# Cross-attention kernel, layer 0: rankings one head pair later, token blocks split straight from PSUM, the output product ahead of the values

## What is computed

```python
score = jnp.einsum('bqhd,bkhd->bhqk', h_q, h_k)
score = score + position_bias[None]
score = jnp.where(m, score, -jnp.inf)
score = jax.nn.softmax(score, axis=-1)
score = jnp.where(m, score, 0.0)
attn = jnp.einsum('bhqk,bkhd->bqhd', score, h_v).reshape(b, lq, H * DH)
out = attn @ w_out.T
return hidden_states + out
```

## Time and profile before

| what | value |
|---|---|
| median of 3 runs | 1880.85 us (1878.38 to 1881.03) |
| profiled execution, own time | 1878.18 us |
| its span in the profile | 1876.3 us |
| mean granted PE clock | 0.985 |
| busy PE / DVE / ACT / POOL | 1791.9 / 1415.9 / 653.5 / 690.5 us |

### The profile page before, as it was taken

One profiled execution on the slowest core, in us unless ns is written; L12 is line 12 of the kernel. 1 busy time (PEld: TensorE's weight loads), 2 busy tenths in 40 slices (PEclk: granted clock), 3 DMA queues, 4 the chain that ended last, 5 costly groups with the idle time before them and its releaser, 6 DMA issues. The chain is left out here.

```text
span 1876.3 us, 29528 instructions
## 1 busy us (share of the span) xinstructions
PE 1791.9 (95%) x10312; PEld 1510.3 (80%) x10312; DVE 1415.9 (75%) x2838; ACT 653.5 (35%) x1785; POOL 690.5 (37%) x457
## 2 busy tenths in 40 slices
PE   7789999999999999997999998879999999999998
PEld 5679889888888988896776664666888888888886
DVE  6777777777777777776536876779778888888886
ACT  5222223333223212332114766531343343343333
POOL 6633344443334343432223002426433333334331
PEclk9989999999999999999999998989999999999999
DMA  3121011111110111120010001110101010100111
GB/s 143 42 72 48 31 50 50 50 50 50 50 50 23 49 40 40 50 77 1 23 45 20 1 26 56 35 42 21 46 25 44 34 34 34 34 34 34 34 35 46
DMA packets 32026, 78.27 MB, mean 42 GB/s; under 512 B 4096, under 2 KB 10944, under 8 KB 31584
## 3 DMA queue, kind: packets, MB, share of 16 engines
q1 hardware_dynamic: 31968, 77.50, 12.6%
HBM read 75.39 MB, written 2.10 MB: 41 GB/s over the span
## 5 line engine op out<-in xcount | busy, mean ns | idle before, releaser
L649 POOL TENSOR_TENSOR l0x_comb<-l0x_neg,l0x_bias 128x1024 f32<-128x1024 bf16 x32 | 70.2, 2194 | 375.4 <-DVE l0x_probs L1048 362.5
L945 ACT ACTIVATE l0x_probs_t<-bank 128x512 f32<-128x512 f32 x32 | 19.1, 597 | 527.5 <-PE bank L789 527.5
L2852 POOL TENSOR_TENSOR l3x_q<-l3x_q,l3x_cross 128x512 f32<-128x512 f32 x64 | 89.7, 1407 | 188.3 <-DVE l3x_q L1823 188.3
L37 PE MATMUL bank<-l0x_w_v_hi,ctx_hi 128*128 128x256 f32 x512 | 145.0, 283 | 0.0
L39 PE MATMUL bank<-l0x_w_v_hi,ctx_lo 128*128 128x256 f32 x512 | 145.0, 283 | 0.0
L38 PE MATMUL bank<-l0x_w_v_lo,ctx_hi 128*128 128x256 f32 x512 | 144.9, 283 | 0.0
L929 ACT ACTIVATE l0x_probs<-l0x_probs,l0x_top 128x129 f32<-128x129 f32 x256 | 99.4, 390 | 65.7 <-DVE l0x_top L1052 65.7
L37 PE MATMUL bank<-ctx_hi,l0x_w_k_hi 128*128 128x512 f32 x256 | 104.7, 409 | 8.3 <-DVE ctx_lo L1130 8.3
L3039 ACT ACTIVATE l3x_probs<-l3x_probs,l3x_top 128x128 f32<-128x128 f32 x256 | 99.1, 389 | 38.1 <-DVE l3x_top L3120 38.0
L1092 DVE TENSOR_TENSOR x<-x,bank 128x512 f32<-128x512 f32 x120 | 82.1, 684 | 37.5 <-PE bank L39 37.5
L37 PE MATMUL bank<-l3x_qin_hi,l3x_w_q_hi 128*128 128x512 f32 x256 | 105.7, 413 | 2.2 <-ACT l3x_v L3073 1.9
(11 more groups left out here) (486 smaller groups left out, 5358.4 us busy)
## 6 DMA issues: line engine op xcount, KB each, us to landing
l0x_raw_k<-L_k_dram SPq DMA_DIRECT2D x32, 256.0 KB, 3.3
l0x_raw_v<-L_v_dram SPq DMA_DIRECT2D x16, 512.0 KB, 3.3
l0x_raw_q<-L_q_dram SPq DMA_DIRECT2D x16, 512.0 KB, 4.2
l0x_raw_o<-L_o_dram SPq DMA_DIRECT2D x16, 512.0 KB, 3.4
l3x_raw<-L_q_dram SPq DMA_DIRECT2D x16, 512.0 KB, 3.2
l3x_raw<-L_o_dram SPq DMA_DIRECT2D x16, 512.0 KB, 3.3
kv_raw<-L_kv_dram SPq DMA_DIRECT2D x8, 512.0 KB, 3.4
l0x_ctx_raw<-ctx_t_dram SPq DMA_DIRECT2D x4, 512.0 KB, 6.0
```

What stands on the lines that cost most here:

```text
L37: pe.matmul(out, lhs[0], rhs[0], start=start, stop=False)
L649: pool.tensor_tensor(comb[:, :, :], neg[:, :, :], bias[:, j:j + 1, :].to_broadcast([P, B, P]), ALU.add).then_inc(comb_ready, 1)
L945: act.activation(probs_t[:, 0:BH, :], bank[6][:, :].rearrange("p (b n) -> p b n", b=BH), ACT.Copy).then_inc(t_act, 1)
L2852: pool.tensor_tensor(dst[:, part], dst[:, part], cross[n][:, :], ALU.add).then_inc(rotated, 1)
```

## The change

- **Rankings.** Pair 0 ranks no more. In pair p the ranking p-1 runs, and the last (15) goes into DVE's part of the feed-forward layer, a step behind each of the eight output tiles (`between(b)`).
- **Even step.** `project_out` stands ahead of the four `value_bank` on PE, and DVE's additions ahead of its value drains; the ranking's first round stands behind the second addition.
- **Blocks.** ACT rounds the transposed x from PSUM right into `xs[0]` (`high_x`), DVE copies the same bank to `xt` and subtracts the low part from PSUM (`copy_x`). The sums are made in another order, two (`T1`, `T2`) before pair 0, two within it; PE waits for two, then for four. Pair 0's queries have a buffer of their own (`raw_q0`), so that pair 1's are loaded at the start and split before pair 0. The mask is turned into `neg` by ACT.
- **Queues.** SP: the mask ahead of x; `load_work(p)` at the end of pair p, where `load_work(p + 1)` stood, and thus one in the last pair, too. ACT: in the last pair `w_o` is split ahead of `copy_probs(h)`.

The diff, cut:

```diff
@@ L0Ffn.vector
-    def vector(self, dve):
+    def vector(self, dve, between):
...
             core.statistics(dve, b)
+            between(b)
@@ l0_layer
-        ITEM = {"k_odd": 0, "v": 2, "out": 6, "p1": 14, ...
+        ITEM = {"k_odd": 0, "out": 2, "v": 10, "p1": 14, ...
-        SUMS = {3: 3, 4: 0, 5: 1, 6: 2}
+        T1, T2, T3, T4 = 4, 5, 3, 6
+        SUMS = {T1: 3, T2: 0, T3: 1, T4: 2}
@@ sync, period
                     if not last:
-                        if first:
-                            sp.wait_ge(ring_full, 10)
-                        else:
-                            sp.wait_ge(q_ready, p)
-                        load_q(p + 1)
+                        if not first:
+                            load_q(p + 1)
                         load_v(p + 1)
                         load_k(p + 1, 1)
                     if first:
-                        sp.wait_ge(xs_ready, L0_BLOCKS)
+                        sp.wait_ge(xs_ready, 4)
                     load_o(p)
                     if not last:
                         load_bias(p + 1, 0)
-                        load_work(p + 1)
+                    if not first:
+                        load_work(p)
@@ gpsimd
-                pool.tensor_scalar(neg[:, :, :], mask_u8[:, :, :], 1.0, -MASKED, ALU.subtract, ALU.mult
-                                   ).then_inc(neg_ready, 1)
                 pool.wait_ge(neg_ready, 1)
                 combine(0, 0)
-                for n in range(3):
-                    pool.wait_ge(xs_hi, n + 1)
-                    pool.tensor_tensor(xs[1][:, n, :, :], x_block(n), as_f32(xs[0][:, n, :, :]), ALU.subtract
-                                       ).then_inc(xs_ready, 1)
+                sum_queries(1)
+                low_queries(1)
@@ tensor, period
                     if not first:
+                        project_out(p - 1, at(p, "out"))
                         pe.wait_ge(v_ready, p + 1)
                         for m in range(4):
                             value_bank(at(p, "v") + m, 4, OUT_BANKS[m], m)
-                        project_out(p - 1, at(p, "out"))
...
-                    if first:
-                        pe.wait_ge(xs_ready, L0_BLOCKS)
                     pe.wait_ge(q_ready, p + 1)
                     block_product(at(p, "p1"), 3, 0, 0, 0)
-                    block_product(at(p, "p6"), 3, 3, 5, 5)
+                    if first:
+                        pe.wait_ge(xs_ready, 2)
+                    block_product(at(p, "p6"), 3, 3, 5, T2)
@@ scalar, period
                         for n in range(3):
                             ffn.high(act, n)
+                        split_high(p, raw_o, w_o, o_loaded, o_hi, at(p, "out") + B)
...
                     copy_probs(h)
@@ vector, before the pairs
+                def copy_x(b):
+                    dve.wait_ge(xt_hi, b + 1)
+                    dve.tensor_copy(xt[:, :, b * P:(b + 1) * P], bank[4 + b % BH][:, :].rearrange("p (c t) -> p c t", c=DC)
+                                    ).then_inc(xt_done, 1)
+                    tokens = slice(b % BH * P, (b % BH + 1) * P)
+                    if b < BH:
+                        dve.tensor_tensor(xs[1][:, 0:2, :, tokens], bank[4 + b][:, :].rearrange("p (k e t) -> p k e t", k=2, e=2),
+                                          as_f32(xs[0][:, 0:2, :, tokens]), ALU.subtract).then_inc(core.xt_copied, 1)
...
@@ vector, period
-                        rank_start(p)
+                        rank_start(p - 1)
+                        for m in range(4):
+                            add_out(at(p, "out"), 2 * m, OUT_BANKS[2 * m % 4])
+                            add_out(at(p, "out"), 2 * m + 1, OUT_BANKS[(2 * m + 1) % 4])
+                            rank_round(p - 1, m)
                         for m in range(4):
                             drain(at(p, "v") + m, OUT_BANKS[m], v[:, 2 * m:2 * m + 2, :])
                             if m < 3:
-                                rank_round(p, m)
-                        for m in range(4):
-                            add_out(at(p, "out"), 2 * m, OUT_BANKS[2 * m % 4])
-                            add_out(at(p, "out"), 2 * m + 1, OUT_BANKS[(2 * m + 1) % 4])
-                            rank_round(p, 3 + m)
-                        rank_end(p)
+                                rank_round(p - 1, 4 + m)
+                        rank_end(p - 1)
...
-                    step_odd(p)
+                    step_odd(p, first)
                     if first:
-                        rank_start(p)
-                        for r in range(ROUNDS + 1):
-                            rank_round(p, r)
-                        rank_end(p)
                         dve.wait_ge(h_added, B)
```

More of the change, by code:

```diff
@@ L509, in l0_layer @@
         heads = pair("heads", [P, 2, T])
-        probs = [sb("probs0", [P, B, P + 1]), sb("probs1", [P, B, P + 1])]
+        probs = [sb("probs0", [P, B, P + 1])]
+        with ExitStack() as early:
+            raw_q0 = core.sb(early, "l0x_raw_q0", [P, 2, DC, P])
+        probs.append(sb("probs1", [P, B, P + 1]))
         idle = sb("idle", [P, 1])
@@ L544, in at @@
             return PER * p - 2 + ITEM[what]
-        OUT_LAST = at(N - 1, "out") + B
+        OUT_LAST = at(N - 1, "v") + 4
         ADDED = OUT_LAST + 1
@@ L570, in load_q @@
                 def load_q(i):
+                    wait(sp, q_ready, i - 1)
                     sp.dma_start(raw_q[:, :, :, :], dram["L0_q"][i, :, :, :, :]).then_inc(q_loaded, 16)
@@ L703, in period @@
                     combine(p, 1)
-                    if not last:
-                        sum_queries(p + 1)
-                        split_low(p + 1, raw_k[0], w_k[0], k_hi[0], k_ready[0])
-                        low_queries(p + 1)
                     if first:
@@ L711, in period @@
                                            ).then_inc(core.rstd_done, 1)
-                        pool.wait_ge(lift_done, 2)
+                    if not last and not first:
+                        sum_queries(p + 1)
+                    if not last:
+                        split_low(p + 1, raw_k[0], w_k[0], k_hi[0], k_ready[0])
+                    if not last and not first:
+                        low_queries(p + 1)
                     if last:
@@ L754, in plain_query @@
                     for c in range(DC):
-                        mm = product(pe, bank[bk][:, :], [raw_q[:, j, c, :]], [xt[:, c, n * HALF:(n + 1) * HALF]],
+                        mm = product(pe, bank[bk][:, :], [raw_q0[:, j, c, :]], [xt[:, c, n * HALF:(n + 1) * HALF]],
                                      c == 0, c == DC - 1)
@@ L979, in _ @@
                     scale_x(b)
-                act.wait_ge(ctx_lo, DC)
+                act.wait_ge(mask_loaded, 16)
+                act.activation(neg[:, :, :], mask_u8[:, :, :], ACT.Copy, bias=MASKED, scale=-MASKED).then_inc(neg_ready, 1)
                 act.wait_ge(shift_done, 2)
@@ L983, in _ @@
                     scale_x(BH + b)
-                    copy_x(b)
+                    high_x(b)
                 split_high(0, raw_k[1], w_k[1], k_loaded[1], k_hi[1], 0)
-                high_x(0)
-                high_x(1)
                 for b in range(BH, B):
-                    copy_x(b)
-                for n in range(2, L0_BLOCKS):
-                    high_x(n)
+                    high_x(b)
+                high_queries(1, 0)
+                high_sum(T1, 1)
+                high_sum(T2, 2)
                 def period(p, first, last):
@@ L997, in period @@
                     exps(h, 0)
-                    if not first:
+                    if first:
+                        high_sum(T3, 3)
+                        high_sum(T4, 4)
+                    else:
                         heads_high(h - 1, 1)
@@ L1014, in period @@
                         split_high(p + 1, raw_v, w_v, v_loaded, v_hi, 6 if first else at(p, "v") + 4)
-                    split_high(p, raw_o, w_o, o_loaded, o_hi, 0 if first else at(p, "out") + B)
+                        split_high(p, raw_o, w_o, o_loaded, o_hi, 0 if first else at(p, "out") + B)
                 pairs(period, act)
@@ L1151, in _ @@
+                for b in range(BH):
+                    copy_x(b)
                 drain(5, 1, v[:, 6:8, :])
+                copy_x(4)
+                copy_x(5)
                 drain(6, 2, q00)
+                copy_x(6)
+                copy_x(7)
                 b11, b21, b22, b12 = (x_block(n) for n in range(4))
                 total = lambda n: x_sum[:, SUMS[n], :, :]
-                dve.wait_ge(core.xt_copied, B)
-                dve.tensor_tensor(total(3), b22, b12, ALU.subtract).then_inc(xs_sum, 1)
@@ L1158, in _, with low_sum @@
[L1158 to L1166 removed]
+                def low_sum(n, order):
+                    dve.wait_ge(xs_hi, order)
@@ L1186, in step_even, with step_odd @@
                     normalise(h, 0)
-                def step_odd(p):
+                def step_odd(p, first):
                     h = 2 * p + 1
@@ L1193, in step_odd @@
```

(13 more changed lines are left out.)

77 lines of the change are left out of this document (42 added, 35 removed).

## The result

The changed kernel takes 1888.32 us (median of 5 runs, 1886.83 to 1891.08); the kernel before takes 1878.93 (median of 5, among them the three shown above), so the change costs 9.4 us. The ratio is 1.005, with a 95% interval of 1.0037 to 1.0063: slower by half a per cent. The forecast was 1882.5 with a range of 1876.5 to 1889, and it put 0.58 on no change and 0.27 on slower. The profiled execution is the one of 1888.32 us.

What follows compares the result with a forecast made beforehand. PE bounds the kernel, busy 1791.9 of 1876.3 us. Terms -12.8 - 6.0 + 4.0 + 14.4 + 0 + 2.0 = +1.6 us gave 1879.8 profiled, plus 2.67 a median of 1882.5; range 1876.5 to 1889.

Steps and rivals of the forecast that it cites:

- B: Pair 0: first scores at 42.3 instead of 40.31, yet pair 1's even scores at 76.9 instead of 82.87; -6.0 us.
- C: Pair 1: new wait for POOL's additions, behind a bias load held in SP's queue; +4 us, ends 0 and 9.7.
- D: Loop pairs: fifth output tile waits for the first addition, which stands behind DVE's negation; +14.4 us.
- E: Last pair: 5.54 us wait for w_o goes, but weights queue behind ranking 14's load; +2 us, ends -0.5 and +6.
- A: Pair 0's ranking goes: pair 1's even step loses a 9.7 us wait and about 3.0 of half clock; -12.8 us.
- one wait a pair, 13 x 1.11: Loop pairs 2 to 14: PE loses 1.11 us once a pair, at the fifth output tile; 14.4 us.
- Pair 15's wait: Last pair: POOL's weight splits come later, so the negation is not held and PE does not wait; 0 us.
- 18 matmuls of 0.23: Last pair's output product: 18 matmuls taking from S+16.4 to S+20.6, S being the start of the last odd scores.
- rival 3: Last pair: late third weight piece and half clock through 18 matmuls; +6 to +8 us there, 1887 to 1889; chance 0.20.
- Rival 1: Loop pairs: no wait at the fifth tile, D vanishes, time 1868 us; chance 0.12.
- Rival 2: Pair 1: no hold, bias early or covered by PE's weighting; C 0.7 to 1, time 1879 us; chance 0.15.
- rival 4: Loop pairs: second wait, on the low heads, or a longer fifth-tile wait; D 20, time 1888 us; chance 0.10.

Runs made afterwards that it cites:

- Experiment 8: Kernel before the change with pair 0's ranking left out, its load and store kept: 1865.7 us, ratio 0.9932.
- experiment 9: Changed kernel with the edits of experiments 1, 2, 5 and 6 together: 1858.38 us, ratio 0.989 to the kernel before.
- experiment 5: Changed kernel with the bias of head 2 loaded ahead of SP's wait for the block sums: 1884.28 us, ratio 1.0025 to the kernel before.
- experiment 1: Changed kernel with rank_start's negation behind the first two output additions instead of ahead of them: 1871.01 us, ratio 0.9951 to the kernel before.
- experiment 3: Changed kernel with the negation on an eighth of the piece (32 of 256 elements), rankings partly other ones: one run, 1887.0 us.
- experiment 7: Changed kernel with POOL's second low split of query weights held until the first output addition: 1869.75 us, ratio 0.9946 to the kernel before.
- experiment 10: Kernel of experiment 9 plus the edit of experiment 7, and the mask loaded behind x: 1865.43 us, ratio 0.9921 to the kernel before.
- Experiment 2: Changed kernel with the last load_work behind the feed-forward weight loads, PE waiting for the last value drain: 1879.3 us, ratio 0.9997 to the kernel before.
- experiment 4: Changed kernel with the values ahead of the output product again on PE and DVE: 1871.2 us, ratio 0.9956 to the kernel before.
- experiment 6: Kernel of experiment 5 with DVE's fourth query tile drain ahead of a block sum in pair 0: 1884.24 us, ratio 1.0024 to the kernel before.

## How the forecast held, and where it was low

The working named each wait that decided, with its releaser and in its place. Its sum was too low: 1.6 forecast, plus 1.2 (B), less 1.1 (C), plus 2.1 (D), plus 2.5 (E), plus 3.7 for which no term stood, is the span's 10.0. The time lies inside the range (1888.3 against 1889), and that is in part luck: the forecast stood on a median of 1880.85 for the kernel before, which the two later runs brought to 1878.93. On that base the same working gives 1880.6 and a range up to 1887.1, and the time would lie outside. Of the chances, the largest stood on no change, and slower came.

- **A, -12.8: right in size.** Experiment 8 measured 11.8 in the step by itself. The changed kernel alone shows only A and C together (-9.9).
- **B, -6.0: measured -4.8.** The first scores came at 43.4, not 42.3: the fourth query tile's drain was queued behind a sum of blocks that took 3.26 us beside POOL's split (the sum before it took 1.23), and the x loads were 0.6 us later. In experiment 9, with the drain ahead of that sum, they came at 42.4. The ends of 0 and +3 held it. A finer test is not to be had from single profiles: over the kernels built on the change the first scores came between 42.4 and 46.0 us.
- **C, +4: measured +2.9**, and experiments 5 and 9 show that its cause is the one named, the bias load queued behind SP's wait. Bias and additions came within 0.8 us of the forecast.
- **D, +14.4: measured +16.5.** The mechanism was right (experiments 1, 3 and 7), and so was the pause, 1.11 us by start to start. The step that failed is "one wait a pair, 13 x 1.11": the price of a pause was taken to be its length. The tiles behind it cost 0.12 to 0.15 more. In experiment 10 this is plainer, with 0.24 us shown and 0.54 lost.
- **Pair 15's wait, 0: right, and for the reason given.** POOL's splits came later (from 859.6 us on, the negation at 834.3), and the even step took 32.3 us. Experiment 2 shows the other side: with the weights early, the wait is there.
- **E, +2: measured +4.5**, inside its ends. The landing, the copy and the 7.4 us wait came as worked out. What failed is "18 matmuls of 0.23": half clock lasted to the end of the output product, 7.1 us instead of 4.1. The forecast had this as part of rival 3 ("if PE's clock is not back by S+16"), and gave it too little. The 7.1 us are the dearest case, too: in the six other kernels that have the long pause (7.5 to 9.5 us) the clock came back before or inside the product, which took 4.2 us once (experiment 4) and 5.6 to 6.0 us five times, and the transposes stood at S+22.0 to S+23.4. So the forecast took the cheapest outcome for the likeliest, and about 1 us of the miss belongs to this profile.
- **No term: the border to layer 1, +2.8.** The forecast assumed that code behind the change keeps its time. The remaining 0.9 us lie in the later layers and were not traced. The cause of the 3.7 us stays open.
- **The rivals.** Rival 3 gave 1887 to 1889, and the time fell there with half of its mechanism (the clock, not a late landing). Rival 1 (1868) is what happens when the addition comes in time: experiments 1 and 7 gave 1871 and 1870. Rival 2 did not occur, rival 4 neither: no other wait stood in the loop.

On why the negation is slow, the Trainium skill (SBUF — State Buffer, "SBUF: two separate sides") says that DVE in certain forms and GpSimd share a port pair as an exclusive lock, which goes to the one that starts first, for its whole instruction. The runs agree: 1.92 us beside POOL's split, 1.81 for an eighth of the size, 0.28 with POOL idle, and additions that read PSUM not held at all. On the burst of weights, the estimate by the Trainium skill's fit (DMA: Bandwidth & Descriptors, "Anatomy of one DMA — SWDGE (gpsimd) path") gave 5.3 us from the first issue; ACT used the third piece 862.24 - 855.65 = 6.6 us behind it. The Trainium skill gives the fit for one transfer on GpSimd's path, and these are several that SP issues one behind another. The measurement decides.

## What to carry to other kernels

When a reordering makes PE use a ring of buffers faster, look at the one instruction of the draining engine that now stands in front of the first drain: moving it behind two additions was worth 17 us of 1888. An instruction that takes longer than elsewhere and whose end lies just behind another engine's end is probably held by that engine; a run with an eighth of its size tells, as experiment 3 did. While it is held its size tells nothing, and an edit that changes when the other engine runs can bring the wait back somewhere else, as experiment 10 did, and as experiment 2 did in pair 15. Price a pause of PE by the length of the whole step with and without it: the bracket in the row is too small, and with half clock behind it far too small.

## What the runs showed of the hardware

- **Same pause, other clock.** Behind the pause at the border to layer 1 (3.09 to 3.13 us in all twelve kernels) the 24 products took 5.5 us in the kernel before and in experiments 6 and 8, 8.3 in the changed kernel and in experiment 9, and 7.2 in the seven others. The length of the pause, which hardly differs, doesn't decide it; what does was not found. Code that a change leaves alone may so differ by 2.8 us between two profiles. Nor need that difference last: from the first of these products to the end of the span are 913.0 us both in experiment 6, where PE stood at half clock from 1014.5 us on for 3.4 us instead, and in the changed kernel.
- **Half clock outlasts the return of work.** In the changed kernel PE had work again from 864.8 on, with a pause of 2.0 us in it, and stayed at 1.2 GHz until 877.
- **Two engines hold each other in turn.** `normalise` takes 3.03 us beside POOL's first split and 1.22 in pair 15, where POOL is idle; it ends 1.07 us behind that split. POOL's second split takes 2.82 us when it begins beside `normalise` and 1.84 when it was moved away; it ends 1.70 us behind `normalise`. The negation takes 1.92 us beside the second split and 0.28 alone, and ends 0.15 us behind it. What each spends behind the other's end (1.07, 1.70 and 0.15 us) is nearly what it takes alone (1.22, 1.84 and 0.28).
